# One run of four products for the values of each step, in place of two half runs of four

## The reference

```python
q, k, v = split(clip(x @ w_qkv.T, -8, 8))      # 32 heads of 16
q, k = layernorm(q) * w + b, layernorm(k) * w + b
scores = einsum('bqhd,bkhd->bhqk', q, k) * 16 ** -0.5
scores = where(causal, scores + slope[h] * (k_pos - q_pos), -inf)
attn = einsum('bhqk,bkhd->bqhd', softmax(scores), v)
out = attn @ w_out.T
```

## The kernel before

| step | 0 | 1 | 2 | 3 | 4 to 8 | 9 | 10 | 11 |
|---|---|---|---|---|---|---|---|---|
| tile of keys | 0 | 1 | 2 | 3 | 0 to 4 | 5 | 6 | 7 |
| columns | 512 | 384 | 256 | 128 | 512 | 384 | 256 | 128 |

## Time and profile before

### The profile page before, as it was taken

One profiled execution on the slowest core, in us unless ns is written; L12 is line 12 of the kernel. 1 busy time (PEld: TensorE's weight loads), 2 busy tenths in 40 slices (PEclk: granted clock), 3 DMA queues, 4 the chain that ended last, 5 costly groups with the idle time before them and its releaser, 6 DMA issues. The chain is left out here.

```text
span 2023.7 us, 26337 instructions
## 1 busy us (share of the span) xinstructions
PE 1916.9 (95%) x10439; PEld 1504.0 (74%) x10439; DVE 856.4 (42%) x1586; ACT 437.1 (22%) x534; POOL 610.3 (30%) x692
## 2 busy tenths in 40 slices
PE   6999999999999999999999869998888999987999
PEld 5888888888888888888888758886653444456887
DVE  5242342432433333424324453313666888725611
ACT  3111111111111111111111121101313666643200
POOL 4322231321312313222300045534720212225532
PEclk9999999999999999999999979998985999998999
DMA  4010100110110100101100112201033233001111
GB/s 157 29 58 29 58 29 29 57 57 10 47 57 29 54 32 30 56 29 57 36 0 16 47 53 83 81 7 69 21 66 51 48 54 55 14 22 47 50 50 68
DMA packets 36521, 93.15 MB, mean 46 GB/s; under 512 B 7200, under 2 KB 11936, under 8 KB 31968
## 3 DMA queue, kind: packets, MB, share of 16 engines
q1 hardware_dynamic: 35172, 89.56, 15.1%
q10 hardware_dynamic: 1276, 2.62, 0.8%
HBM read 75.89 MB, written 2.10 MB: 39 GB/s over the span
## 5 line engine op out<-in xcount | busy, mean ns | idle before, releaser
L146 PE MATMUL a_ps<-a_xh_h,a_w_h 128*128 128x512 f32 x768 | 307.4, 400 | 4.3 <-POOL a_w_l L270 2.9
L148 PE MATMUL a_ps<-a_xh_h,a_w_l 128*128 128x512 f32 x768 | 301.3, 392 | 0.0
L147 PE MATMUL a_ps<-a_xh_l,a_w_h 128*128 128x512 f32 x768 | 300.7, 391 | 0.0
L60 POOL TENSOR_TENSOR tick<-neg_half 128x1 f32<-128x1 f32 x48 | 24.6, 513 | 615.7 <-PE a_ps L148 615.7
L390 DVE TENSOR_TENSOR x<-x,a_ps 128x1024 f32<-128x1024 f32 x64 | 78.2, 1221 | 259.9 <-PE a_ps L148 259.9
L1153 ACT ACTIVATE a_pr<-a_ps 128x1024 f32<-128x1024 f32 (+1 forms) x192 | 153.1, 812 | 88.3 <-PE a_ps L1366 71.4
L146 PEld LDWEIGHTS a_ps<-a_xh_h,a_w_h 128*128 128x128 f32 x768 | 145.0, 189 | 32.5 <-issue 3.3
L148 PEld LDWEIGHTS a_ps<-a_xh_h,a_w_l 128*128 128x128 f32 x768 | 144.6, 188 | 30.4
L147 PEld LDWEIGHTS a_ps<-a_xh_l,a_w_h 128*128 128x128 f32 x768 | 144.9, 189 | 27.9
L146 PE MATMUL a_ps<-a_w_h,a_xh_h 128*128 128x512 f32 x352 | 145.0, 412 | 8.7 <-POOL a_w_l L251 5.9
L1386 PE MATMUL a_ps<-a_K,a_Q 64*128 64x512 f32 (+2 forms) x384 | 136.8, 448 | 14.1 <-DVE a_mx L1261 11.5
(11 more groups left out here) (180 smaller groups left out, 3651.9 us busy)
## 6 DMA issues: line engine op xcount, KB each, us to landing
a_raw<-in_a_wqkgv SPq DMA_DIRECT2D x30, 1024.0 KB, 4.9
f_raw<-in_f_w SPq DMA_DIRECT2D x33, 320.0 KB, 2.9
a_raw<-in_a_wout SPq DMA_DIRECT2D x32, 256.0 KB
f_raw<-in_f_w SPq DMA_DIRECT2D x32, 256.0 KB, 2.6
a_cst<-in_a_cst SPq DMA_DIRECT2D x32, 129.0 KB, 2.0
a_K<-a_k_h SPq DMA_DIRECT2D x54, 64.0 KB
a_Q<-a_q_h SPq DMA_DIRECT2D x52, 64.0 KB
a_raw<-in_a_wqkv SPq DMA_DIRECT2D x3, 1024.0 KB, 4.8
```

The lines of the kernel that those rows point to most:

```text
L60: nc.gpsimd.tensor_tensor(top["tick"][:, :], top["neg_half"][:, 0:1], top["neg_half"][:, 1:2], ALU.mult)
L146: nc.tensor.matmul(out, w_hi, x_hi, start=start, stop=False)
L147: nc.tensor.matmul(out, w_hi, x_lo, start=False, stop=False)
L148: return nc.tensor.matmul(out, w_lo, x_hi, start=False, stop=stop)
```

## The change

`values` takes every step as whole. Part 0 issues the four products over all columns of the step and raises `values_done`; part 1 returns at once. The waits, the slots and the pieces stay.

```diff
             def values(g, n, part):
 
                 kt, q0, width = STEPS[n]
-                whole = kt == 0 or width == P
+                whole = True
                 if part == 0:
                     pe.wait_ge(s("score_taken"), score_at(g, n, 1) + 1)
```

## The result

The changed kernel takes 2030.2 us in the median of 9 runs (2020.1 to 2038.1), the kernel before 2022.3 in 9 runs beside them. The ratio is 1.0042 with a 95% interval of 1.0023 to 1.0062: slower by 0.4%. Forecast were 2016 and a gain of 6 us.

The account below looks back on a forecast made before the run. PE is busy for 95% of the span, but in regular quads the bound alternates between PE and DVE. Regular quads -3.0, quad 0 -2.3 and quad 7 -0.9 give about -6 us: 2016 us, range 2007 to 2027.

Parts of the forecast that it names:

- The clock: TensorE's rise from 1.2 to 2.4 GHz: moved 5 us either way, it costs or gives about 2.5 us.
- The price of a merge: Joining two half blocks of values saves PE one fixed part, 0.12 us, and one entry, 0.20 us: 0.32 us.
- The regular quad: Quads 1 to 6, each four heads in 24 slots: -0.5 us a quad, -3.0 us for six.
- Steps 1 and 2: Regular quad: the 512-wide piece comes some 0.4 us sooner, and the gain is kept: -0.4 us.
- Steps 5 to 8: Regular quad, slots 13 to 19: longer blocks delay DVE, step 5 +0.42, steps 6 to 8 more, about +0.7 us together.
- Slot 20: Regular quad: it loses its 0.56 us block, PE's part of a 0.68 us wait of DVE: -0.65 us.
- Steps 9 and 10: Regular quad: DVE waits for PE throughout; -0.35 us, of which slot 23 gives 0.2 back: net -0.15 us.
- Quad 0 and the last: Quad 0: PE is the bound, -1.5 and -0.8 at 1.2 GHz, together -2.3 us; quad 7, without pieces: -0.9 us.
- Starvation: Rival, 12%: three banks do not cover a 0.98 us block; slots 13, 15, 17, 19 each lose 0.42: +4 us or 2034.
- the drain named from the Trainium skill: Before a block of values: a change of tiling mode drains the engine, which the 0.20 us entry looks like.

Follow-up runs that it names:

- The filler: Changed kernel plus four zero-operand products in each emptied slot: 2037.2 us; in slots 8 and 0 only, all steps but 5 and 6 merged: 2018.5 us.
- the bunched kernel: Against the kernel before, both halves of each step issued in part 0 one behind the other, not merged: 2030.7 us, ratio 1.0032.
- the wide kernel: Against the kernel before, only steps 5 to 8 made whole besides 0, 3, 4 and 11: 2028.2 us, ratio 1.0017.

## Why the prediction was wrong

**The clock.** "It widens the range and moves no chance" is the step that failed. I looked only at the rise in quad 0, and put at nothing what another order of PE's work does in the regular quads, where the clock had been at 2.4 GHz until the end of quad 6. A lapse of 3.4 us costs about 1.4 us. The runs of the changed kernel take 6.7 us more in the mean than the 93 of the kernel before whose clock is on record (2030.5 against 2023.8; against the 9 beside them, the medians differ by 8), and they have 15 to 16 us more at 1.2 GHz. At the price of a lapse that gives 6 us. A line through all runs of all kernels, each kernel with its own level, gives 0.35 us for each us at 1.2 GHz, 5.5 us for the 15 to 16; at equal clock the changed kernel lies about 1 us above the kernel before. The filler shows that the cause is in what PE is given: in the one profile of each of the two kernels with it the lapses are gone, and the clock of their runs is back. It is not the columns, for the bunched kernel has all of them and lapses too. What exactly sets off a lapse is open, be it when PE works, how often it changes between kinds of blocks, or its short waits: steps 1 and 2 alone have none and 1, 2, 7, 8 have two, with the same short stretch; one or two profiles of a kernel do not settle that.

**The price of a merge**, "one fixed part and one entry", 0.12 + 0.20 us. The fixed part belongs to the entry and exit of a block and not to its four products, since 16 records cost what 8 do. The sum fits the filler: a block of 128 columns by these terms is 0.34 + 0.20 = 0.54 us, and where the filler costs anything it costs 0.45 to 0.53. The place was right: emptied slots gain, filled ones lose.

**The regular quad**, forecast -0.5 us, measured +0.13 at full clock (19.99 + 11.04 against 19.42 + 11.48) in quads 1 to 4. By its terms:
- Steps 1 and 2: -0.4 forecast, -0.43 to -0.44 measured. Right, also in that it is kept.
- Steps 5 to 8: +0.7 forecast, and +1.3 measured ahead of slot 20, 1.12 of it in DVE's waits. The timeline of steps 5, 6 and 7 in the changed kernel, to be laid beside the earlier trace rows:

```profile
1625.79 1.05 PE L1425 MATMUL a_ps<-a_pr,a_v 128*17 128x512 f32 x8
...
1626.78 0.49 PE L1386 MATMUL a_ps<-a_K,a_Q 64*128 64x512 f32 x1
...
1627.31 1.29 DVE L1261 TENSOR_REDUCE a_mx<-a_ps 128x1 f32<-128x512 f32 x2 [0.60 <-PE a_ps L1386]
...
1629.08 1.05 PE L1425 MATMUL a_ps<-a_pr,a_v 128*17 128x512 f32 x8
...
1630.60 0.69 DVE L1257 CUSTOM_DVE_ANT_0 a_masked<-a_ps,a_mask 128x512 bf16<-128x512 f32 x1 [0.71 <-PE a_ps L1386]
...
1633.72 0.56 DVE L1257 CUSTOM_DVE_ANT_0 a_masked<-a_ps,a_mask 128x384 bf16<-128x384 f32 x1 [0.25 <-PE a_ps L1386]
```

  The wait of DVE behind step 6 in the kernel before:

```profile
1632.07 0.69 DVE L1257 CUSTOM_DVE_ANT_0 a_masked<-a_ps,a_mask 128x512 bf16<-128x512 f32 x1 [0.27 <-PE a_ps L1386]
```

  Step 5 came as worked out: 0.60 where 0.17 had been, +0.43. Step 6 was undersized: 0.71 against 0.27, +0.44, not 0.25. Step 7 costs a wait of 0.25, not 0.05. Beside these 1.12 of waits DVE's own work ahead of slot 20 takes 0.17 longer, 0.10 of it in one L1265 (0.42 us instead of 0.32); its last piece ahead of slot 20 starts 1.29 us later in the long stretch than before.
- Slot 20: the wait of 0.68 is gone, as forecast (-0.65).
- Steps 9 and 10: -0.15 forecast, -0.11 to -0.12 measured where they are merged without steps 7 and 8 (19.31, 19.30). In the changed kernel the two waits of DVE behind slot 20 are 0.22 and 0.57 where 0.48 and 0.36 had been, so -0.05 is left.

The sum is -0.44 + 1.29 - 0.68 - 0.05 = +0.12. So the terms were right in sign and place, and that of the wide steps was too small by 0.6. In six quads that is 3.6 us, and turns the gain of 3 into a loss of half a us; measured are +1.1 for quads 1 to 6 with the three lapses taken off, since quads 5 and 6 are not like the others (the long stretch of quad 6 alone lost 0.46, at a lower clock, 0.89 against 0.92).

**Quad 0 and the last.** From slot 12 of quad 0 to slot 3 of the next 22.34 us stand against 22.96, -0.6 where -1.5 was forecast. Other kernels tell by which steps: with 5 and 6 merged alone this stretch takes 23.30, 0.34 more, where a merge was taken to save 0.32; with 7 and 8 it takes 22.15, 0.8 less, and with 9 and 10 22.86, 0.1 less. So the merges of steps 5 and 6 cost time even here, where PE was taken for the bound. The part of quad 0 at 1.2 GHz and the last quad gave 0.2 each, not 0.8 and 0.9. With +1.1, -0.6, -0.2 and -0.2 the heads are as long as before at full clock, +0.1 us; the three lapses make it the 4.3 that were measured.

**The rivals.** Starvation, with 12%, is the mechanism of the 0.7 us in the long stretch of the wide kernel, and its reason (narrow pieces as cover) is borne out by steps 5 and 6 having all of it. Its condition, that all of slots 13, 15, 17 and 19 lose 0.42, held for the first two only, and its total of +4 with the gains of the narrow steps counted was too high for the quads at full clock. "Against it: the banks are full, mostly with wide pieces" was wrong for the two slots that count. Of the drain named from the Trainium skill ("TensorEngine Tiling (Array Packing)", "Key Properties") the runs agree in so far as only blocks in slots of their own cost extra (0.99 us for 16 records in one block as for 8); that it is a drain, no run shows.

## What to carry to other kernels

Where two engines are coupled through few buffers, moving work into bigger lumps costs as soon as one lump lasts longer than what the buffers hold at that place; look at the sizes of what is buffered just ahead of each lump, and merge only where they are large. When PE's work is put in another order, treat its clock as a term of its own: work out the change at equal clock and the change of the clock separately, and compare the clock of all runs, not of one profile. Here a gain that was lost to the clock was kept with idle products in two slots behind which DVE was the bound; in all eight emptied slots the same products cost more than they gave.

## What the runs showed that was not expected

The time follows the mean granted clock closely: the runs of the changed kernel lie between 2020.1 us at 0.970 and 2038.1 at 0.959. The clock fell for 3.4 us, and once for 13 us, in stretches in which PE is shown busy for over 90% of the time. In both profiles of the changed kernel the clock fell once more behind the heads, in code that is the same as before; that the change brings this about is likely, but no run tests it. Adding sixteen groups of four products made a kernel faster, by 6 us in the median (2024.5 to 2018.5 us, in different sets of runs) and by 4 us when each is measured against the kernel before beside it (0.9998 and 0.9979).
